# Expert stage two packed by rows: the 96-row rests of ten experts in eight units of 128

## The reference

```
scores = softmax(x @ gate_w)                       # 256 x 8 experts, the best 2 kept -> comb
g      = silu(x @ w_gate[e]) * (x @ w_up[e])       # 256 x 352 for each expert e
routed = sum_e comb[:, e] * (g @ w_down[e])        # 352 -> 512
shared = silu(x @ sw_gate) * (x @ sw_up) @ sw_down # width 704 = 2 x 352
out    = x + routed + shared
```

## Time and profile before

| | |
|---|---|
| median of 3 runs | 1444.71 us (1443.2 to 1445.79) |
| the profiled execution, its own time | 1442.28 us |
| its span (first to last instruction) | 1440.5 us |
| granted TensorE clock, mean | 0.996 of full |
| busy: PE, DVE, ACT, POOL | 96%, 80%, 66%, 10% |
| DMA moved | 194.50 MB in 46337 packets |

### The profile page before, as it was taken

How to read it: one execution, slowest core, us unless ns; L and a number is a source line. 1 busy time by engine, 2 the same in 40 slices (tenths; PEclk the granted TensorE clock), 3 DMA queues, 4 the chain that set the end, 5 groups by cost and what they waited for, 6 DMA issues and landing times. The chain is left out here.

```text
span 1440.5 us, 27413 instructions
## 1 busy us (share of the span) xinstructions
PE 1381.4 (96%) x10740; PEld 842.4 (58%) x10740; DVE 1154.9 (80%) x1672; ACT 944.7 (66%) x1770; POOL 138.7 (10%) x171
## 2 busy tenths in 40 slices
PE   4999999999999999998999899999989889999998
PEld 2433333333333333333458899999967764568998
DVE  5999999999999999997486766666658457877665
ACT  1688888888888888888274555555523632775453
POOL 4122222121122222120000000000000000000000
PEclk9999999999999999999999999999999999999999
DMA  7544655555544545543206554555355532104540
GB/s 178 146 112 96 172 139 111 140 139 125 119 116 108 119 99 110 104 69 59 88 1 259 195 191 175 178 189 198 135 212 212 234 124 110 67 1 162 197 182 32
DMA packets 46337, 194.50 MB, mean 135 GB/s; under 512 B 16984, under 2 KB 17408, under 8 KB 34176
## 3 DMA queue, kind: packets, MB, share of 16 engines
q1 hardware_dynamic: 46032, 192.77, 45.6%
q10 hardware_dynamic: 192, 0.20, 0.1%
HBM read 167.69 MB, written 21.83 MB: 132 GB/s over the span
## 5 line engine op out<-in xcount | busy, mean ns | idle before, releaser
L530 DVE TENSOR_REDUCE pm<-bank 128x1 f32<-128x1024 f32 x512 | 621.3, 1221 | 14.8 <-PE bank L611 9.3
L589 ACT ACTIVATE probs<-bank 128x512 f32<-128x512 f32 x1024 | 554.5, 598 | 97.4 <-PE bank L630 91.5
L611 PE MATMUL bank<-kst,qst 48*128 48x512 f32 x1024 | 371.1, 452 | 21.7 <-DMA qst<-qsplit 19.9
L630 PE MATMUL bank<-qst,kst 52*128 52x512 f32 (+1 forms) x1024 | 372.4, 448 | 1.5 <-DVE pm L530 0.8
L647 PE MATMUL bank<-probs,vext 128*32 128x256 f32 x3968 | 316.7, 391 | 0.0
L630 PEld LDWEIGHTS bank<-qst,kst 52*128 52x128 f32 (+1 forms) x1024 | 153.0, 185 | 210.9 <-ACT probs L589 182.0
L1296 PE MATMUL bank<-e_xhi,e_hi 128*128 128x256 f32 (+1 forms) x784 | 222.8, 284 | 4.7 <-DVE e_lo L1231 4.2
L1296 PE MATMUL bank<-e_xlo,e_hi 128*128 128x256 f32 (+1 forms) x784 | 222.4, 284 | 0.0
L1296 PE MATMUL bank<-e_xhi,e_lo 128*128 128x256 f32 (+1 forms) x784 | 222.4, 284 | 0.0
L647 PEld LDWEIGHTS bank<-probs,vext 128*32 128x32 f32 x3968 | 78.1, 108 | 181.2 <-ACT probs L589 91.3
L611 PEld LDWEIGHTS bank<-kst,qst 48*128 48x128 f32 x1024 | 149.8, 186 | 29.2 <-DMA qst<-qsplit 19.9
(11 more groups left out here) (220 smaller groups left out, 1520.1 us busy)
## 6 DMA issues: line engine op xcount, KB each, us to landing
raw<-wall SPq DMA_DIRECT2D x34, 1536.0 KB, 6.6
kst<-kscratch SPq DMA_DIRECT2D x192, 128.0 KB, 4.5
raw<-wall SPq DMA_DIRECT2D x10, 2304.0 KB, 8.5
kscratch<-ksplit SPq DMA_DIRECT2D x15, 1024.0 KB, 4.7
kraw<-ctx_rows SPq DMA_DIRECT2D x16, 512.0 KB, 6.3
vraw<-ctx_vt SPq DMA_DIRECT2D x16, 512.0 KB, 7.3
ctxT<-ctxT SPq DMA_DIRECT2D x8, 1024.0 KB, 11.8
nat<-ctx_chunks SPq DMA_DIRECT2D x6, 1024.0 KB, 21.8
```

What stands on the lines that cost most here:

```text
L530: nc.vector.tensor_reduce(pm[:, h % 2, r % 4, c:c + 1], bank[:, 2 * (r % 2):2 * (r % 2) + 2, :], AX.XY, ALU.max).then_inc(pre_reduced, 1)
L589: nc.scalar.activation(probs[:, (XST * k + n) % PR, :], bank[:, S_BANK[k][n], :], ACT.Exp, scale=XSCALE).then_inc(probs_ready, 1)
L611: ins = nc.tensor.matmul(bank[:, 2 * (r % 2) + j, :], qst[64 * j:64 * j + KR, h, tt * P:tt * P + P], kst[64 * j:64 * j + KR, h % 2, c * 51 ...
L630: nc.tensor.matmul(bank[:, S_BANK[k][n], :], kst[64 * j:64 * j + rows, h % 2, m * P:m * P + P], qst[64 * j:64 * j + rows, h, :], start=Tru ...
```

## The change

The ten third units of 96 rows hold 960 rows. The change puts them into eight units: seven of 128 rows and one of 64. Unit 2 of slot n = 0 to 7 (`j == 2`) is made of the pieces that `Packed.pieces` lists as (first row, end row, expert, its unit, its first row there). Slot 8 takes expert 8's two full units and, as its third, the first full unit of expert 9; slot 9 has one unit, the second of expert 9. So e1 has 28 units instead of 30. The weights in HBM stay as they are; the packing is done by the loads. A slot with two pieces is loaded by five transfers (one 128 x 12 KB for its two full units; for each piece one of gate and up weights, as 128 x 8 runs of 96, 64 or 32 floats, and one of down weights, as 96, 64 or 32 rows of 2 KB), slot 7 by three, slot 8 by two, slot 9 by one. Where a unit holds rows of two experts, DVE multiplies each range of rows by its own gate. The waits for the spread gates come one unit earlier (after units 4 and 10). The cuts stay 128 x 1536 whatever the rows. Stage e0 goes through the new class `Plain`, which gives the loads, waits and rows as they were.

```diff
+class Plain:
...
+    def shares(self, n, j):
+        return [(0, P, n)]
...
+class Packed:
+    def __init__(self, n, width, raw, raw_loaded, wall):
+        assert n == 10 and width == 2 * P + 96
+        self.units, self.last = 3, 1
+        self.raw, self.raw_loaded = raw, raw_loaded
+        self.wall = [wall[e].rearrange("p (u w) -> p u w", u=3) for e in range(n)]
+    def pieces(self, n, j):
+        if n == 8 and j == 2 or n == 9:
+            return [(0, P, 9, n - 8, 0)]
+        if j < 2:
+            return [(0, P, n, j, 0)]
+        q, k = divmod(n, 3)
+        e = 4 * q
+        if n == 7:
+            return [(0, 64, 9, 2, 32)]
+        return [[(0, 96, e, 2, 0), (96, P, e + 1, 2, 0)],
+                [(0, 64, e + 1, 2, 32), (64, P, e + 2, 2, 0)],
+                [(0, 96, e + 3, 2, 0), (96, P, e + 2, 2, 64)]][k]
+    def rows(self, n, j):
+        return self.pieces(n, j)[-1][1]
+    def shares(self, n, j):
+        return [(lo, hi, e) for lo, hi, e, u, a in self.pieces(n, j)]
+    def transfers(self, n):
+        return 1 + 2 * len(self.pieces(n, 2)) if n < 8 else 10 - n
+    def load(self, sp, n):
+        raw, loaded = self.raw[n % 2], self.raw_loaded[n % 2]
+        if n < 9:
+            sp.dma_start(raw[:, 0:2, :], self.wall[n][:, 0:2, :]).then_inc(loaded, 16)
+        if n >= 8:
+            j = 2 if n == 8 else 0
+            sp.dma_start(raw[:, j, :], self.wall[9][:, n - 8, :]).then_inc(loaded, 16)
+            return
+        up = 2 * DC * P
+        for lo, hi, e, u, a in self.pieces(n, 2):
+            b = a + hi - lo
+            sp.dma_start(raw[:, 2, 0:up].rearrange("p (m c) -> p m c", c=P)[:, :, lo:hi],
+                         self.wall[e][:, u, 0:up].rearrange("p (m c) -> p m c", c=P)[:, :, a:b]).then_inc(loaded, 16)
+            sp.dma_start(raw[lo:hi, 2, up:], self.wall[e][a:b, u, up:]).then_inc(loaded, 16)
+    def loaded(self, n, s):
+        return 16 * sum(self.transfers(m) for m in range(n % 2, n + 1, 2))
...
-def experts(g, k, name, E, width, choose, gate_w, gate_loaded, raw, raw_loaded, wall, cb, parts_at, rings, AHEAD, DONE, C_UNIT,
+def experts(g, k, name, E, choose, gate_w, gate_loaded, plan, cb, parts_at, rings, AHEAD, DONE, C_UNIT,
             first_loads, later_loads, out=None):
     nc, sem, bank, X = g.nc, g.sem, g.bank, g.X
-    rows = [min(P, width - u * P) for u in range(-(-width // P))]
-    U = len(rows)
+    U, raw = plan.units, plan.raw
     N = E + 2
+    units_in = lambda n: plan.last if isinstance(n, int) and n == N - 1 else U
+    TOTAL = U * (N - 1) + plan.last
+    ungated = [u for u in range(2 * U) if all(e < 2 for lo, hi, e in plan.shares(*divmod(u, U)))]
+    FREE = len(ungated)
...
     def over_units(eng, step):
...
         for n in range(N - 4, N):
-            for j in range(U):
+            for j in range(units_in(n)):
                 step(n, n % 4, j)
...
         if j == 0:
-            act.wait_ge(raw_loaded[s % 2], (n - s % 2) * 8 + 16)
+            act.wait_ge(plan.raw_loaded[s % 2], plan.loaded(n, s))
...
                 sp.wait_ge(w_lo, U * (n - 1))
-                sp.dma_start(raw[n % 2][:, :, :].rearrange("p u w -> p (u w)"), wall[n]).then_inc(raw_loaded[n % 2], 16)
+                plan.load(sp, n)
...
             def step(n, s, j):
-                b, u, r = place(s, j), n * U + j, rows[j]
-                shared = isinstance(n, int) and n < 2
+                b, u, r = place(s, j), n * U + j, plan.rows(n, j)
+                gated = [share for share in plan.shares(n, j) if not (isinstance(share[2], int) and share[2] < 2)]
                 dve.wait_ge(silu_ready, u + 1)
-                if not shared:
-                    c = cb[0:r, bass.ds(n - 2, 1), :].rearrange("p e t -> p (e t)")
-                    nc.vector.tensor_tensor(silu[0:r, b, :], silu[0:r, b, :], c, ALU.mult).then_inc(weighted, 1)
-                    dve.wait_ge(weighted, u - (2 * U - 1))
+                if gated:
+                    for lo_r, hi_r, e in gated:
+                        c = cb[lo_r:hi_r, bass.ds(e - 2, 1), :].rearrange("p e t -> p (e t)")
+                        ins = nc.vector.tensor_tensor(silu[lo_r:hi_r, b, :], silu[lo_r:hi_r, b, :], c, ALU.mult)
+                    ins.then_inc(weighted, 1)
+                    dve.wait_ge(weighted, u - FREE + 1)
                 if not (isinstance(n, int) and u < 2):
                     dve.wait_ge(act_hi, u - 1)
                 nc.vector.tensor_tensor(acts[0:r, b % 2, :], silu[0:r, b, :], bank[0:r, b, T:2 * T], ALU.mult).then_inc(act_made, 1)
...
-                if isinstance(n, int) and n == 1 and j == U - 1:
+                if isinstance(n, int) and u == FREE - 1:
                     dve.wait_ge(c_first, 16)
-                if isinstance(n, int) and n == 3 and j == U - 1:
+                if isinstance(n, int) and u == FREE + 2 * U - 1:
                     dve.wait_ge(c_spread, 16)
 
             over_units(dve, step)
-            dve.wait_ge(down_done, U * N)
+            dve.wait_ge(down_done, TOTAL)
...
+        plan0 = Plain(E0 + 2, I0, raw0, raw0_loaded, ins["wall0"])
+        plan1 = Packed(E1 + 2, I1, raw1, raw1_loaded, ins["wall1"])
...
-            load_raw1(sp, 0)
+            plan1.load(sp, 0)
 
         def later_e(sp):
-            load_raw1(sp, 1)
+            plan1.load(sp, 1)
...
-                   [(wo1_loaded, 16)], loads_e, later_e, (rings1, raw1, raw1_loaded, 3, 16, 2))
+                   [(wo1_loaded, 16)], loads_e, later_e, (rings1, raw1, raw1_loaded, 3, 16, 2, plan1.loaded(0, 0)))
```

More of the change, by code:

```diff
@@ L794, in self_attention @@
     TE = RE - (1 if late else 0)
-    first_ahead, pieces = ahead[4:]
+    first_ahead, pieces = ahead[4:6]
     def ends_tile(m):
@@ L999, in rest_ahead @@
             def rest_ahead(piece):
-                rings, raw, _, U, _, _ = ahead
+                rings, raw, _, U, _, _, _ = ahead
                 (k, j), half = divmod(piece // 2, U), piece % 2
@@ L1081, in high_ahead @@
             def high_ahead(piece):
-                rings, raw, raw_loaded, U, _, _ = ahead
+                rings, raw, raw_loaded, U, _, _, loaded = ahead
                 (k, j), half = divmod(piece // 2, U), piece % 2
                 cols = slice(WU // 2 * half, WU // 2 * half + WU // 2)
-                act.wait_ge(raw_loaded[k], 16)
+                act.wait_ge(raw_loaded[k], loaded)
                 ins = nc.scalar.copy(rings.hi[k][j][:, cols], raw[k][:, j, cols])
@@ L1115, in _ @@
                     high_ahead(i - first_ahead)
+class Plain:
+    def __init__(self, n, width, raw, raw_loaded, wall):
+        self.units, self.last = width // P, width // P
+        self.raw, self.raw_loaded, self.wall = raw, raw_loaded, wall
+    def rows(self, n, j):
+        return P
+    def shares(self, n, j):
+        return [(0, P, n)]
+    def load(self, sp, n):
+        sp.dma_start(self.raw[n % 2][:, :, :].rearrange("p u w -> p (u w)"), self.wall[n]).then_inc(self.raw_loaded[n % 2], 16)
+    def loaded(self, n, s):
+        return (n - s % 2) * 8 + 16
@@ L1217, in later @@
         q, jj = divmod(j + d, U)
-        if isinstance(n, int) and not 0 <= n + q < N:
+        if isinstance(n, int) and not (0 <= n + q < N and jj < units_in(n + q)):
             return None
@@ L1275, in down @@
             def down(n, s, j, last=False):
-                u, r = n * U + j, rows[j]
+                u, r = n * U + j, plan.rows(n, j)
                 b = place(s, j)
@@ L1310, in _ @@
             for d in range(DLAG, 0, -1):
-                down(*later(N - 1, (N - 1) % 4, U - 1, 1 - d), last=d == 1)
+                down(*later(N - 1, (N - 1) % 4, plan.last - 1, 1 - d), last=d == 1)
         @block.scalar
@@ L1722, in loads_a @@
                 sp.dma_start(dst, src).then_inc(small_loaded, 16)
+        plan0 = Plain(E0 + 2, I0, raw0, raw0_loaded, ins["wall0"])
+        plan1 = Packed(E1 + 2, I1, raw1, raw1_loaded, ins["wall1"])
         def loads_b(sp):
             for n in range(2):
-                sp.dma_start(raw0[n][:, :, :].rearrange("p u w -> p (u w)"), ins["wall0"][n]).then_inc(raw0_loaded[n], 16)
+                plan0.load(sp, n)
         def first_d(sp):
@@ L1738, in loads_d @@
             sp.dma_start(wq1[:, :, :], ins["wq1"]).then_inc(qkv1_loaded, 16)
-        def load_raw1(sp, n):
-            sp.dma_start(raw1[n][:, :, :].rearrange("p u w -> p (u w)"), ins["wall1"][n]).then_inc(raw1_loaded[n], 16)
         def loads_e(sp):
@@ L1760, in perceiver @@
                    [(w_attn0_loaded, 64)], [smalls], [(w_attn0_loaded, 64)], loads_b, None,
-                   (rings0, raw0, raw0_loaded, 2, 1, 8))
-        experts(g, 2, "e0", E0, I0, "sigmoid", gate0, [smalls], raw0, raw0_loaded, ins["wall0"], cb0, 32,
+                   (rings0, raw0, raw0_loaded, 2, 1, 8, 16))
+        experts(g, 2, "e0", E0, "sigmoid", gate0, [smalls], plan0, cb0, 32,
                 rings0, 4, 4, 2, lambda sp: None, ahead_d)
@@ L1772, in perceiver @@
```

(4 more changed lines are left out.)

## The result

The changed kernel takes 1436.12 us in the median of 7 runs (1433.3 to 1437.64), the kernel before 1443.92 in 7 runs beside it (1441.29 to 1445.79). The ratio is 0.995, 95% interval 0.9939 to 0.996: 7.8 us faster. The profiled execution of the changed kernel took 1436.34 us, its span is 1434.6.

What follows compares the result with a forecast made beforehand. PE bounds stage e1, at nearly the same time for padded and full units. Two units fewer give -7.8 us, cuts, gates and loads nothing: 1444.71 - 7.8 = 1436.9 us, range 1435.0 to 1441.6 with the spread case.

Steps and rivals of the forecast that it cites:

- PE's units: Stage e1: PE's 28 units instead of 30 take 119.2 us instead of 127.0, a gain of 7.8 us.
- Cuts and gates: Stage e1, ACT and DVE: two units' cuts fewer and five second gate multiplies of 0.46 us, all hidden: nothing.
- The short runs: Loads in e1: 27 ns per short run, DMA engines busy 7.9 us a load, landing after 10.7 us, in time.
- SP's issues: SP's queue in e1: four further issues a load at about 0.62 us each, 2.5 us, hidden under the first transfer.
- one of my signs of being wrong: Profile of e1: SP's issues of short runs taking far more than 0.6 us would speak against the forecast.
- The play of the spread: SP's queue before load 3: the gates' store is delayed 2.2 us, which SP's wait from 1319.96 to 1322.20 covers: nothing.
- The slower one: Loads in e1: short runs bound the stage, PE waiting from 71 ns a run; at 100 ns 1457.5 us; chance 8%.
- The spread rival: Start of e1: load 2 delays the gates' store, SP issues load 3 late, PE waits 4.7 us once: 1441.6; chance 8%.

Runs made afterwards that it cites:

- e1: Not a run: the stage of experts that the change packs, 30 units before and 28 after; from its second pair of units 121.2 us before, 113.74 after.
- e0: Not a run: the other stage of experts, whose loads, waits and rows the change leaves as they were; splitting its gate spread gave 1430.36 us.
- what the change adds: Kernel before, 30 units, with all ten third units loaded by five transfers a slot and gated in two row ranges: 1442.85 us, ratio 1.000.
- the saving without the short runs: Changed kernel with its 28 units packed in the layout of the weights, each slot one long transfer: 1434.45 us, ratio 0.9946.
- halves: Changed kernel with each gate-and-up piece loaded by two transfers of half the columns, 4096 short runs a slot: 1434.57 us, ratio 0.9945.
- quarters: Changed kernel with each gate-and-up piece loaded by four transfers of a quarter of the columns, 8192 short runs a slot: 1441.57 us, ratio 0.9998.
- eighths: Changed kernel with each gate-and-up piece loaded by eight transfers of an eighth of the columns, 16384 short runs a slot: 1466.05 us, ratio 1.0157.
- loads and gates alone: Kernel before, 30 units, with the change's five-transfer loads and double gate multiplies for all ten third units: 1442.85 us, ratio 1.000.
- the two with quarters: Changed kernel with gate-and-up pieces loaded in quarters: 1441.57 us; the same with e1's gate spread issued by GpSimd instead of SP: 1438.01 us.
- the filled 128-row kernel: Change packed in the weights' layout, 64-row unit as 128 rows, 15 unread matmuls before e0's first gate and up product: 1435.81 us, ratio 0.9949.
- the two with the split spread: Change with e0's gate spread cut in two, 28 experts' gates after load 4: 1430.36 us; also packed in the weights' layout, 64-row unit as 128 rows: 1430.97 us.

## Why the prediction was right

**PE's units.** Right in kind and nearly in size, and shown by both halves: what the change adds is free (1.000), and the saving without the short runs is the whole saving. The forecast was 7.8 us and 1436.9; the profile has 7.5 behind the start, and the median is 1436.12. That the medians differ by just 7.8 is luck: their interval runs from 5.8 to 8.8 us. The 0.3 that are missing in the profile come from the 64-row unit: I took 4.09 us by carrying 128 to 96 on to 64, and it is 2.73 + 1.58 + 0.19 = 4.50, 0.41 more. Against that, a full unit takes 4.26 us and not 4.265, some 0.1 less over 27 of them.

**Cuts and gates.** Nothing, as forecast. DVE's double multiply takes 0.85 us, and ACT still waits 1.1 us for PE's down product after it.

**The short runs.** I took 27 ns each; it is 26. That this came so close is partly luck, as it was put together from a window of other transfers and an allowance for the bytes. A load of five transfers issued from 1350.27 keeps the engines busy for 68.8% of the 12 us behind it, 8.3 us against my 7.9. The DMA view of 1350 to 1362 us, with the last of the five transfers:

```profile
q1 hardware_dynamic: 2384, 2.36, 68.8%
...
raw<-wall SPq DMA_DIRECT2D x1, 64.0 KB, 6.0
```

That last transfer was issued at 1354.24 and took 6.0 us to land, so the load was in 10.0 us after its first issue; I had 10.7. The split of a short run's time into a fixed part and bytes, in the expectations for halves and quarters, was wrong, and it mattered only for the quarters.

**SP's issues.** This term was mis-sized, and one of my signs of being wrong, issues of far more than 0.6 us, came true although the forecast held. Four further issues at 0.62 us were to take 2.5 us; load 3 took from 1322.44 to 1330.91, 8.5 us. It cost nothing, because the load still landed in time and the next thing on SP's queue comes later, at 1337.13. The quartered kernel fell over it.

**The play of the spread.** I gave 2.2 us; the spread was issued by 1321.9 in place of 1319.96, in a stage that began 0.24 us later, so 1.7 us were used, and load 3 went out at 1322.44, 0.24 us after that of before.

**The rivals.** The slower one did not come: it needed 128 short runs at 71 ns, 9.1 us an engine, and there are 3.3. Forced with eighths, 10.6 us an engine, it does. The rule of the Trainium skill ("DMA: Bandwidth & Descriptors", Specifications) that transfers below 512 B miss line rate agrees with the trace as far as that goes: 256 bytes in 26 ns are 10 bytes a ns, and a long packet moves 24 on one engine; nothing here shows a read before the write. The spread rival is the one that exists: in e1 it was kept off (load 3's last issue ends at 1330.91, ACT wants the load at 1337.01), and in e0 it is there before and after the change.

**The clock.** Not in the forecast. In the profiled execution of the change the clock granted to PE went to half for 3.4 us at the start of e1, where the profile of before has it at full:

```profile
1309.00:1310.00 1.00, 0.73 (x4) 0.71 0.00 0
1310.00:1311.00 1.00, 1.00 (x6) 0.50 0.00 0
...
1312.00:1313.00 1.00, 1.00 (x7) 0.58 1.07 188
```

One stretch of the profile of before:

```profile
1310.00:1311.00 1.00, 1.00 (x11) 1.00 0.06 16
```

Half is 1.2 of 2.4 GHz. Of the other profiles one (loads and gates alone, with 30 units) has the same 7.50 us there, and the others 6.0, so it seems to belong to the execution and not to the change. The fall in e0 varies too. Around 800 us the clock is at half for about 6.8 us in six profiles (before, the change, loads and gates alone, halved, and the two with quarters) and for about 3.4 in four; it does not fall in the filled 128-row kernel, with 3.4 us of idle, nor in the two with the split spread. Part of what single executions of one kernel differ by can be this.

## What to carry to other kernels

Where the engine that bounds a stage takes nearly the same time for a padded unit as for a full one, count the units: packing the rests is worth their number times the unit's time, and the packing may be left to the loads as long as the DMA engines and the issuing queue both stay within the stage's pace. Price the two separately, per short run and per issue, and look at what stands behind the long issue on its queue. And look for a wait where a large transfer that is not urgent is queued ahead of a load that is: here that was worth 5.6 us, where the change itself was worth 7.8.

## What the hardware showed that I had not expected

- A transfer of short runs holds the queue that issues it, and more so the transfer behind it; why is not shown. Single issues in e1 took up to 4.4 us, where the transfers of before take 0.33. A load's issues, first to last, took 6.2 us with 2048 short runs (1337.13 to 1343.30; 8.5 for load 3) and 12.1 with 8192 (1343.81 to about 1355.9). The longest in the change is in a1, in load 0, and cost nothing because SP had nothing else to issue until 1228.90:

```profile
1178.70 13.70 SPq L1187 DMA_DIRECT2D raw<-wall  x1
```

- A down product with 64 rows of contraction among those of 128 costs a gap: both it and the matmuls behind it took 0.19 us more, and with 128 rows both gaps were gone. Between 128 and 96 rows no such gap shows in the earlier trace rows.
- The clock's fall came in different places in executions of the same program's stages, after PE had been idle or had run only the small gate matmuls. In the change it fell within 3.9 us of idle, at about 797.4 us, and was half until about 804.3; in the filled 128-row kernel it did not fall behind 3.4 us of idle; with the idle cut to 0.6 us it did not fall in either profile. At the start of e1 it fell, in 2 of 13 profiles, behind the 16 small matmuls of the gates.
